# Depthwise stage: column-by-column numbering of a patch, residual and output copied in runs of 2 KB

## What is computed

```python
def _L3_conv_ref(x, A_kernel, B_kernel, gate_A_kernel, gate_B_kernel, W_out, b_out, T):
    # x is group-normed; kernels are 7 x 7 per channel, circular
    gate_A = sigmoid(ifft_real(gA_f * x_f))
    gate_B = sigmoid(ifft_real(gB_f * x_f))
    b_spatial = ifft_real(B_f * x_f)
    ...
    h_final = jnp.exp(log_h[-1])      # a scan over T = 8 equal steps
    return h_final @ W_out + b_out
x = x + _L3_conv_ref(_gn(x), ...)
```

## Time and profile before

| | us |
|---|---|
| median of 3 runs | 5107.27 |
| lowest and highest | 5104.38 to 5115.54 |
| the profiled execution | 5114.19 |
| its span, first to last instruction | 5112.3 |
| depthwise stage in it | 4150 to 5039 |
| origin patch | 5039 to 5112 |

### The profile page before, as it was taken

One profiled execution on the slowest core, in us unless ns is written; L12 is line 12 of the kernel. 1 busy time (PEld: TensorE's weight loads), 2 busy tenths in 40 slices (PEclk: granted clock), 3 DMA queues, 4 the chain that ended last, 5 costly groups with the idle time before them and its releaser, 6 DMA issues. The chain is left out here.

```text
span 5112.3 us, 108138 instructions
## 1 busy us (share of the span) xinstructions
PE 4593.3 (90%) x36006; PEld 3426.1 (67%) x36006; DVE 3447.8 (67%) x10158; ACT 2799.9 (55%) x6303; POOL 2608.4 (51%) x1909
## 2 busy tenths in 40 slices
PE   6999999999999997769999899997399979999972
PEld 5777777777777775356777576764144459898871
DVE  6888888888888886425666566663388835565554
ACT  0888888888888884024333333333044425555551
POOL 1999999999999993022233132320144401222221
PEclk8999999999999998889999899998699989999985
DMA  7222222222222225962222222217577789999972
GB/s 295 68 73 75 76 73 75 76 73 75 76 73 75 76 74 200 385 204 91 69 67 69 81 69 68 69 58 291 208 225 235 235 298 324 331 337 327 331 224 52
DMA packets 826726, 789.33 MB, mean 154 GB/s; under 512 B 62816, under 2 KB 703033, under 8 KB 817625
## 3 DMA queue, kind: packets, MB, share of 16 engines
q1 hardware_dynamic: 804266, 740.90, 46.3%
q10 hardware_dynamic: 18304, 28.26, 1.5%
q0 software_dynamic: 3616, 13.35, 0.7%
HBM read 574.59 MB, written 207.68 MB: 153 GB/s over the span
## 5 line engine op out<-in xcount | busy, mean ns | idle before, releaser
L309 POOL TENSOR_TENSOR at_bias<-at_tri,at_mask 128x1024 f32<-128x1024 f32 x512 | 1215.5, 2374 | 27.3 <-DMA at_mask<-in_L_conv_mask_bias_dram 11.2
L427 ACT ACTIVATE at_probs<-at_neg_s,at_neg_max 128x256 f32<-128x256 f32 x2048 | 871.2, 505 | 0.7 <-DVE at_neg_max L478 0.7
L478 DVE CUSTOM_DVE_ANT_0 at_neg_s<-at_p_s,at_bias 128x256 f32<-128x256 f32 x2048 | 760.0, 418 | 7.6 <-PE at_p_s L350 2.9
L301 POOL TENSOR_TENSOR at_paired_t<-at_probs_t 128x512 f32<-128x512 f32 x512 | 656.6, 1282 | 9.6 <-ACT at_probs_t L419 5.4
L361 PE MATMUL at_p_t<-all_ident,at_probs 128*128 128x128 f32 x4096 | 628.6, 276 | 0.6 <-DVE at_probs_t L486 0.4
L1733 PE MATMUL dw_p_conv<-dw_xw,dw_wts 128*128 128x128 f32 x4096 | 507.8, 276 | 70.1 <-issue 50.9
L946 ACT ACTIVATE ml_h<-ml_p,l_b 128x512 f32<-128x512 f32 x384 | 263.9, 687 | 554.6 <-PE ml_p L905 554.6
L361 PEld LDWEIGHTS at_p_t<-all_ident,at_probs 128*128 128x128 f32 x4096 | 476.0, 141 | 131.7 <-issue 104.1
L1834 POOL TENSOR_TENSOR dw_xr<-dw_xr,all_b_plain 128x512 f32<-128x512 f32 x128 | 190.7, 1490 | 711.8 <-DMA dw_xr<-x3t 711.8
L1047 POOL TENSOR_TENSOR ml_x2t<-ml_z,ml_xb 128x512 f32<-128x512 f32 x128 | 163.6, 1278 | 734.3 <-DVE ml_z L1013 734.3
L1733 PEld LDWEIGHTS dw_p_conv<-dw_xw,dw_wts 128*128 128x128 f32 x4096 | 479.1, 190 | 87.6 <-issue 87.2
(11 more groups left out here) (230 smaller groups left out, 9208.1 us busy)
## 6 DMA issues: line engine op xcount, KB each, us to landing
dw_wts<-patch_w SPq DMA_DIRECT2D x256, 512.0 KB, 8.1
dw_xw<-planes SPq DMA_DIRECT2D x128, 528.0 KB, 6.2
sp_xs<-x SPq DMA_DIRECT2D x128, 512.0 KB, 9.2
planes<-pw_plane SPq DMA_DIRECT2D x128, 264.0 KB, 2.9
in_xs<-in_x_dram SPq DMA_DIRECT2D x32, 1024.0 KB, 7.7
at_xs<-in_x_dram SPq DMA_DIRECT2D x256, 128.0 KB, 2.4
at_kvs<-in_L_conv_kv_x_dram SPq DMA_DIRECT2D x256, 128.0 KB, 2.6
at_mask<-in_L_conv_mask_bias_dram SPq DMA_DIRECT2D x256, 128.0 KB, 3.2
```

What stands on the lines that cost most here:

```text
L301: pool.tensor_tensor(paired_t[:, n % 2, part], probs_t[:, n % 3, part, 0], probs_t[:, n % 3, part, 1], ALU.add).then_inc(paired, 1)
L309: pool.tensor_tensor(bias[:, n % 2, part], tri[:, part], mask[:, n % 4].unsqueeze(1).broadcast_to((128, 4, COLS)), ALU.add).then_inc(maske ...
L427: e = act.activation(probs[:, h, qh, :], neg_s[:, n % 2, h, qh, :], ACT.Exp, bias=neg_max[:, n % 2, i:i + 1], scale=-1.0)
L478: t = dve.tensor_tensor_reduce(neg_s[:, n % 2, h, qh, :], p_s[h][:, qh, :], bias[:, n % 2, i, :], -1.0, 3.0e38, ALU.add, ALU.min, neg_max[ ...
```

## The change

Three things in two functions. The spots are numbered column by column, spot = ox x 8 + oy, in the weights (L1163) and in the choice of the projection's operand (L1754). A projected tile then has 4 neighbouring columns, not rows, in its four matmuls, and rows y to y + 3 on its partitions: partition d x 32 + a holds row y + d of patch a, with four neighbouring pixels of 512 B one after another. And residual and output of a tile are copied by one DMA each, of 128 partitions with runs of 4 x 512 B = 2 KB; the counts in the waits go from 64 (four DMAs of 16) to 16.

```diff
@@ row_taps_and_patch_weights, spread_taps
-                    oy, ox = divmod(spot + i, PATCH)
+                    ox, oy = divmod(spot + i, PATCH)
@@ depthwise_layer, load_residual and store
-                cells = x3t[r // 2, x:x + PX, r % 2 * 64:r % 2 * 64 + 64].rearrange("a (y d) c -> d a y c", d=PATCH)
-                for d in range(4):
-                    sp.dma_start(xr[d * PX:(d + 1) * PX, w % 4], cells[(1 - x) * SHIFT + d][:, y:y + 4]).then_inc(r_loaded[w % 4], 16)
+                cells = x3t[r // 2, x:x + PX, r % 2 * 64:r % 2 * 64 + 64].rearrange("a (y d) c -> y a (d c)", d=PATCH)
+                first = (1 - x) * SHIFT * CH
+                sp.dma_start(xr[:, w % 4].rearrange("p d c -> p (d c)"),
+                             cells[y:y + 4, :, first:first + 4 * CH]).then_inc(r_loaded[w % 4], 16)
...
-                for d in range(4):
-                    sp.dma_start(out[0, r * PATCH + y:r * PATCH + y + 4].rearrange("y (a d) c -> d a y c", d=PATCH)[x + d],
-                                 outs[d * PX:(d + 1) * PX, w % 4]).then_inc(stored[w % 4], 16)
+                sp.dma_start(out[0, r * PATCH + y:r * PATCH + y + 4].rearrange("y (a d) c -> y a (d c)", d=PATCH)[:, :, x * CH:(x + 4) * CH],
+                             outs[:, w % 4].rearrange("p d c -> p (d c)")).then_inc(stored[w % 4], 16)
...
-                sp.wait_ge(stored[s], 64 * (total // 4))
+                sp.wait_ge(stored[s], 16 * (total // 4))
@@ project
-                    spot = (y + i) * PATCH + x
+                    spot = (x + i) * PATCH + y
@@ the additions of POOL and DVE
-                pool.wait_ge(r_loaded[w % 4], 64 * (w // 4 + 1))
+                pool.wait_ge(r_loaded[w % 4], 16 * (w // 4 + 1))
...
-                    dve.wait_ge(stored[w % 4], 64 * (w // 4))
+                    dve.wait_ge(stored[w % 4], 16 * (w // 4))
```

## The result

The changed kernel takes 5280.91 us (median of 4 runs, 5275.07 to 5294.91) where the kernel before, on the same chip, takes 5111.41 (5104.38 to 5119.53): ratio 1.0333, 95% interval 1.0311 to 1.0354. It is slower, as forecast, but by 170 us and not by 324: 5281 lies under the low end of the range, 5380. The profiled execution takes 5275.07 us for a span of 5272.8.

A forecast was written before the change was run, and what follows sets the result against it. DMA was taken to bound the depthwise stage, PE 0.53 us behind. With both copies on four engines, +303, +4 and +17 sum to +324 us: 5438 by the profile, 5431 as median, range 5380 to 5650.

The forecast's parts named there:

- The load on four engines: Depthwise stage: the new residual load, DRAM outermost count 4 against 128 partitions, runs on four of 16 engines, 64 KB each.
- the 127 rows: Copies in L1275: a 127-row piece ran on one engine while 126 rows spread, taken as showing how copies are dealt.
- The store on four engines: Depthwise stage: the new output store, outermost count 4, runs on the same four engines, another 64 KB each per unit.
- The rate: Busiest engines in the depthwise stage: 24.0 GB/s for windows and weights, 24.9 for residual and output, 9.40 us a unit.
- +303: Steps 10 to 110 of the depthwise stage, all copies together: 101 steps x 3.00 us more, +303 us.
- the +4 of steps 6 to 9: Depthwise steps with windows, weights and residual but no output: 6.76 us against 5.69 each, +4 us.
- The tail, +17: Steps 111 to 137, 23 loads and 27 stores on four engines: 132 us against 115, +17 us.
- That is what runs of 512 B cost: Depthwise steady stretch before the change: 512 B runs of residual and output lower the rate from 384 to 330 GB/s.
- the first rival: Depthwise copies use all 16 engines, DMA falls behind PE: -54 us, 5053 us; chance 0.10.
- PE's floor, 5.87 us: Depthwise stage: PE works 5.87 us a unit without a gap, setting the unit if DMA falls behind it.
- the clock rival: Depthwise stage: PE's granted clock drops to 0.50 and binds at 11.7 us a unit, about 5665 us; chance 0.03.
- SP, the bounds of the weights' order, the waits of POOL and DVE: Depthwise stage: fewer SP issues, weight groups issued in time, later residual landings for POOL and DVE: no effect on time.

The follow-up runs named there:

- e1: Changed kernel with the residual load cut into four DMAs of 32 partitions, output still one DMA: 5120.37 us, 1.0022 against the kernel before.
- e2: Changed kernel with the residual loaded by two DMAs of 64 partitions, DRAM count 2 each: 5590.28 us, 1.0943 against the kernel before.
- e4: Changed kernel with the output written to a scratch tensor whose rows are 4 KB longer: 5480.85 us, 1.0729 against the kernel before.
- e3: Changed kernel with both residual load and output store split into four DMAs of 32 partitions, 2 KB runs: 5108.74 us, 1.0015 against the kernel before.
- e14: As e11, but its single residual DMA cut into runs of 512 B: 5035.82 us, 0.9865 against the kernel before.
- e12: As e11, but the residual loaded by four DMAs of 32 neighbouring partitions each: 5114.15 us, 1.0026 against the kernel before.
- e16: As e12, but each of the four residual DMAs fills every fourth partition instead of 32 neighbours: 5032.39 us, 0.9851 against the kernel before.
- e13: Changed kernel with tile partitions numbered patch first (a x 4 + row), hid laid out for it, four softplus operations instead of one: 5054.51 us, 0.9881 against before.
- e8: e1 with the residual loaded for the first four tiles only: 5019.83 us, 0.9818 against the kernel before.
- e5: Changed kernel with the residual's DMA issued from ACT instead of SP: 5278.66 us, 1.0333 against the kernel before.
- e11: Changed kernel with each residual tile read as 256 KB contiguous from image x, one DMA of 128 partitions: 5032.91 us, 0.9854 against the kernel before.
- e7: e1 with the output DMA's direction turned round, loading from the image into the output ring: 5165.38 us, 1.0103 against the kernel before.

## Why the prediction was right in its sign and wrong in its size

- *The load on four engines:* right, and shown by e1, e2 and the table. That the 127 rows say how unequal counts are dealt, the step called the largest risk, held.
- *The store on four engines:* this step failed. "Its outermost count is 4" was read off the way the code writes the pattern. For the load it is so: patches of `x3t` lie 129 x 512 B = 66,048 B apart, rows within a patch 4 KB. For the output the two dimensions have one pitch and count as 128. The sum took 131,072 B for the two copies on each of the four engines where it is 64 KB + 16 KB = 81,920 B. e4 is the kernel the forecast had costed: 5481 us against 5431, unit 9.69 against 9.40.
- *The rate:* mis-sized. 24.0 to 24.9 GB/s were taken for an engine that carries more than the others; 22.5 to 23.8 were measured. By the prediction's rates the corrected sum would be 4.14 + 81,920 B/24.9 = 7.43 us a unit, +104 us in 101 steps; 8.05 us were measured. So the forecast's +303 went wrong by -199 for the store's engines and by +63 for the rate, and +167 between the first and the last window load is what is left (the +4 of steps 6 to 9 lies in the same stretch and can't be told apart). Of the rate itself it is open how much is idle time: SP, which fills the engines' queue, waits 2.4 us a unit for PE in the changed kernel; in e2 it waits 0.5 us a unit, at 23.1 GB/s.
- *The tail, +17:* wrong by the same step. The 23 loads and 27 stores put 23 x 64 + 27 x 16 KB = 1.95 MB on each of the four engines, 87 us at 22.5 GB/s, which fits into the 115 us of the earlier trace rows; measured -5. In e4, with both on four, it is 5484.3 - 5258.9 = 225.4 us from the last window load to the end, +28: there the term is real.
- *"That is what runs of 512 B cost":* wrong, and with it the price of the first rival. The fall from 384 to 330 GB/s was blamed on the new runs' length; but e3 has runs of 2 KB in both copies and the old time, and e14 loads runs of 512 B at 352 GB/s. What the runs show instead is a price on loads onto blocks of neighbouring partitions (e12 against e16). With all 16 engines the time is 5109 to 5120 when the blocks stay and 5031 to 5036 when they go. That the complete kernel without blocks, e13, takes 5054 and so meets the rival's 5053 is luck: its unit is 5.74 us and not 5.87.
- *PE's floor, 5.87 us:* mis-sized. It was one unit's last end minus its first start, and the ends are modelled: in the earlier trace rows the row of 4600.19 ends 0.16 us after the next one starts. From start to start, without the DMA's gap, e8 has 5.54 us on the mean.
- *What the profile was to show:* the rate 263 GB/s where 220 stood, the share 0.84 where 0.58 stood, units of 8.1 for 9.4, packets under 2 KB fewer by 144,896 (703,033 to 558,137) where 98,000 stood; the clock 0.92 inside 0.75 to 0.95, so the clock rival had no part. Stages before unchanged. The gap on PE is 1.6 us a unit where 3.5 stood, and PE waits for windows where weights were named. The rate and the units follow from the store's engines and the rate of the busiest one. The share does not: counted as the prediction does, with the store on 16 engines, it would be (4 x 8.05 + 12 x 4.82)/(16 x 8.05) = 0.70, and in e4, the kernel that the forecast had costed, 0.67 stands where 0.57 would; why it reads higher is open. The packets were a miscount: 98,304 is by how many the runs grow fewer (768 x 128), but all 1024 x 128 = 131,072 runs of 512 B leave the class under 2 KB, since none of the new ones is in it, and 13,824 small packets go with them; that makes 144,896.
- *SP, the bounds of the weights' order, the waits of POOL and DVE:* at nothing, and so they were: e5 takes the residual out of SP's order without a change in time, and in e1 all of it stands at 1.0022.

## What to carry to other kernels

Before two copies are called equal, write down the pitch of each DRAM dimension: dimensions that follow one another at one pitch count as one, and it is the outermost of what is left, on both sides, that deals the copy to the engines; then cost the unit by what the busiest engine carries. A load into SBUF should reach all the partitions, or a spread of them, and not blocks of 32 or 64 neighbours: here that was worth 1.6%, and for the same load the length of runs (512 B or 2 KB) and the number of DMAs (one or four) nothing. Where a share near 1 goes with a falling rate, ask where the bytes go before blaming their size.

## What the hardware showed unexpectedly

- Loads onto blocks of 32 or 64 neighbouring partitions slow everything beside them: 329 and 324 GB/s at a share of 1.04 and 1.05, against 352 at 0.97 for the same bytes with the partitions spread; the weights, which fill all partitions, land in 9.4 us (e12) and not in 7.0 (e16, as many DMAs) or 5.8 (e11, one). Whether stores from such blocks cost as well was not taken apart: e3, with both cut by four, is no slower than e1.
- In this stage each DMA leaves one small packet on every engine that takes part (the counts of seven kernels agree exactly), so the page's count of packets under 512 B tells on how many engines a copy ran.
- An engine that carries more than the others moves 22.5 to 23.8 GB/s in the steady stretch, near the 24.0 of sixteen equal ones that load windows and weights alone. As the mixture differs and the queue may run empty at times, these are no measure of what one engine can do.
- Loads alone (e7, 304 GB/s) were slower than loads with stores (e1, 326 GB/s) of the same bytes. Why is open; no run took it further.
